# Divides moved behind the maxima in the short experts, and two output biases added by a matmul of 33 rows

## The chip, the core and the metric

The kernel runs on one core of a Trainium2 chip. The core has five engines: TensorE (PE, with its weight loads PEld), VectorE (DVE), ScalarE (ACT), GpSimd (POOL) and SyncE (SP), which here only issues DMAs. They run side by side and wait for each other on semaphores. The metric is the device time of one execution in microseconds (us), as the median of several executions.

## What is computed

A graph layer is followed by a layer of four experts. Each of 1250 rows goes to two of the four, and an expert attends only over the rows it was given. Cut to what matters here:

```python
def _expert(xf, mask, ln1_w, ln1_b, ipw, ipb, opw, opb, ln2_w, ln2_b, w1, b1, w2, b2):
    h = _ln(xf, ln1_w, ln1_b)
    q, k, v = jnp.split(h @ ipw.T + ipb, 3, axis=-1)      # 8 heads of 64 columns
    scores = jnp.einsum('htd,hsd->hts', q, k) / jnp.sqrt(D)
    a = jax.nn.softmax(jnp.where(mask[None, None, :], scores, NEG), axis=-1)
    o = jnp.einsum('hts,hsd->htd', a, v).transpose(1, 0, 2).reshape(T, E)
    o = o @ opw.T + opb
    x1 = xf + o
    h2 = _ln(x1, ln2_w, ln2_b)
    m = jax.nn.gelu(h2 @ w1.T + b1, approximate=False) @ w2.T + b2
    return x1 + m
```

The two output biases of the title are `opb` and `b2`, each 512 numbers added to every row.

## The kernel before

The graph layer comes first and takes 332 us. Routing follows, up to 421.5 us: it ranks the rows, makes a list for each expert, and scatters the rows into the lists in DRAM. Then the four experts run one after the other. An expert's rows are tiles of 128. What code an expert runs (its "arm") depends on how many tiles it has. Experts 0, 1 and 3 have four tiles here and run a **short** arm, written out without loops. In experts 0 and 1 the four tiles form two groups of queries, of 128 and of 384 columns (`nq` is 2); in expert 3 they form one group of 512 (`nq` is 1). Expert 2 has ten tiles and runs a **long** arm with a loop over pairs of heads.

Heads are numbered u = 0 to 7 and come in pairs j = u // 2. For a head, TensorE makes scores (L1481) of which VectorE takes each row's maximum (`maxima_of`, L2143, then L2147), TensorE turns the maxima into a row (L1492), ScalarE copies it (L1037), TensorE makes the scores again, transposed and less the maxima (L1506, L1508), ScalarE takes the exponentials (L1057), and TensorE sums values with them (L1522). ScalarE copies sums and denominators out to `o_pair` and `den` (L1049, L1050), and VectorE divides (`divide_of`: L2157 to L2160) into `oT`. Between these, TensorE projects the queries and keys of the pairs to come (`side_of`, L1467), ScalarE adds their bias (L1029, L1031) and VectorE splits them into a high and a low half (`split_of`, L2125 to L2129) and copies the second head's part (`second_of`, L2134 and L2135).

The engines' programs are fixed lists, so the order of the code is the order of the work. In TensorE's `short_head(u)` the first two scores of head u+1 stand early; the third has to wait until VectorE has read the first, because only two banks hold scores. So when VectorE is late with head u+1's first maximum, TensorE stops inside head u. VectorE's order in the short arm is `short_pair(j)`, printed below. After it `divide_of(3, s)` closes the heads, and the out-projection starts.

GpSimd makes the low halves of the weights from ScalarE's high halves (L562), copies values, and adds the biases: a DMA fills `row_par` with a bias on all 128 partitions, `add_bias` adds `opb` to the expert's input rows `x1` (L697) while the heads run, and after the second layer norm has read a tile GpSimd adds `b2` to it (L789). VectorE's `residual` waits for the first (`s_xb`), and its `part` for the second (`s_b2`).

`product(bank, lhs, rhs, chunks)` is TensorE's matmul in float16 halves, three passes over the chunks: 12 matmuls for a tile of the out-projection, 6 for a tile of the last product. An expert's tail is the out-projection (`project_out`), residual, layer norm, two products with the GELU between them, and the sum into `total_rows`. In the profile `x1` and other views of one memory are called `x_mem`.

Of the kernel before, what the change touches and what calls it, by code (L numbers as in the profile page):

```python
# [8 lines left out]
ALU = mybir.AluOpType  # L9
# [45 lines left out]
SHORT = 512  # L55
UP = 5
# [97 lines left out]
def program(nc, x, src, dst, gnn_w, gnn_par, gate_w, gate_b, ew, epar_d, erow, out):  # L154
    stack = ExitStack()
    with stack:
# [132 lines left out]
        row_par = sb("row_par", [P, D], F32)  # L289
# [103 lines left out]
        s_xb = sem("s_xb")  # L393
# [29 lines left out]
        s_b2 = sem("s_b2")  # L423
# [37 lines left out]
        def _(sp):  # L461
# [48 lines left out]
            sp.wait_ge(s_econst, 10)  # L510
# [8 lines left out]
            def expert_sp(e, shape):  # L519
# [26 lines left out]
                biased.skip(nt)  # L546
                sp.wait_ge(s_xb, biased.at(0))
                sp.sem_inc(s_idle, 1)
                sp.dma_start(row_par[:, :], erow[bass.ds(e, 1), 1, :].partition_broadcast(P)).then_inc(s_rp, 16)
                biased.settle()  # L550

            load_rows(0)
            biased = Tally(sp, "sp_biased", 0)
# [4 lines left out]
        def _(pool):  # L558
# [87 lines left out]
            nc.gpsimd.memset(total_rows[:, :, :], 0.0).then_inc(s_econst, 1)  # L646
            pool.wait_ge(s_power, 1)
# [20 lines left out]
            normed = Tally(pool, "pool_normed", 0)  # L668
# [7 lines left out]
            def expert_pool(e, shape):  # L676
# [45 lines left out]
                if shape.short:  # L722
# [7 lines left out]
                    add_bias()  # L730
# [14 lines left out]
                else:  # L745
# [5 lines left out]
                    add_bias()  # L751
# [26 lines left out]
                for p in range(shape.np):  # L778
# [6 lines left out]
                    if p == 0:  # L785
                        pool.wait_ge(s_rp, e * 32 + 32)
# [4 lines left out]
                normed.skip(nt)  # L791
# [16 lines left out]
                for r in (copied, stats, normed, summed, added, gathered, splits, returned_up, seconds):  # L808
                    r.settle()
# [1575 lines left out]
```

## Time and profile before

| what | value |
|---|---|
| median of 3 runs (lowest to highest) | 1335.82 us (1334.84 to 1337.59) |
| the profiled execution | 1336.74 us |
| its span | 1334.7 us |
| granted TensorE clock, mean | 0.884 |
| chain that ended last, by engine | PE 62%, DVE 16%, issue 11%, ACT 5%, POOL 3% |

| stretch, us | what | length | PE busy | DVE busy | ACT busy | POOL busy | clock |
|---|---|---|---|---|---|---|---|
| 332.0 to 421.5 | routing | 89.50 | 29.53 | 38.06 | 18.59 | 54.06 | 0.52 |
| 421.5 to 577.9 | expert 0, short | 156.40 | 111.19 | 100.15 | 72.20 | 58.67 | 0.87 |
| 577.9 to 725.8 | expert 1, short | 147.90 | 108.11 | 95.29 | 64.90 | 53.95 | 0.87 |
| 725.8 to 1173.1 | expert 2, long | 447.30 | 383.87 | 271.89 | 177.81 | 77.28 | 0.93 |
| 1173.1 to 1334.7 | expert 3, short | 161.60 | 122.62 | 86.53 | 57.01 | 40.59 | 0.88 |

The span is what the profiler saw of one execution, and the execution's own time is 2.0 us longer. Busy time is time in which an engine was inside an instruction. The clock is the share of 2.4 GHz that TensorE was granted: 1.0 is 2.4 GHz and 0.5 is 1.2 GHz. A row of a timeline below gives the start and the length of an instruction, or of several alike in a row (x4), and in brackets how long the engine had been idle and which engine's instruction ended that.

### The profile page before, as it was taken

Reading aid. Unit: us, or ns where it says so; the run is one execution under the profiler, and the core shown is the slowest. Engines: PE = TensorE matmul, PEld = TensorE weight load, DVE = VectorE, ACT = ScalarE, POOL = GpSimd, SP = SyncE. Lnnn points to the kernel's source line nnn. Section 1 sums busy time; section 2 is a strip of 40 time slices with the busy share of each in tenths; the row PEclk is TensorE's granted clock in tenths of the full one; section 3 lists DMA queues with packets and bytes.
Section 4 is the critical chain, followed back from the end, with each engine's and each line's share of the span. In section 5 each row is a group of like instructions: output and inputs, shape, how many; then the busy total and the mean of one; then the engine's idle time right before and its main releaser. Section 6 shows DMA issues by size and latency. Waiting matters only on the chain.

```text
span 1334.7 us, 19087 instructions
## 1 busy us (share of the span) xinstructions
PE 1025.8 (77%) x4940; PEld 571.0 (43%) x4941; DVE 749.8 (56%) x1557; ACT 453.7 (34%) x843; POOL 375.2 (28%) x340
## 2 busy tenths in 40 slices
PE   1987699998801876677776888979799779978874
PEld 1654477777800333333334433434344335533323
DVE  5395425441462368745685465674856537835654
ACT  1301121221312355234625423434434452235522
POOL 2102324441366163414342033000000125413212
PEclk9987799998555988889977888989999989989978
DMA  4291000000427114221333010000000312110010
GB/s 147 62 292 43 1 2 0 0 0 1 156 66 236 70 48 146 66 85 32 111 108 123 6 61 4 1 0 0 0 0 7 113 48 64 66 63 1 9 31 33
DMA packets 33792, 76.71 MB, mean 57 GB/s; under 512 B 6373, under 2 KB 6671, under 8 KB 33433
## 3 DMA queue, kind: packets, MB, share of 16 engines
q1 hardware_dynamic: 25405, 58.05, 14.0%
q0 software_dynamic: 8000, 15.44, 4.0%
q10 hardware_dynamic: 288, 2.10, 0.4%
q8 instruction: 39, 0.64, 0.2%
q14 instruction: 60, 0.49, 0.1%
HBM read 52.72 MB, written 24.13 MB: 58 GB/s over the span
## 4 chain that ended last, share of the span: by engine, by line
PE 62%; DVE 16%; issue 11%; ACT 5%; POOL 3%; DMA 1%; DVEq 1%; SPq 0%; ACTq 0%; POOLq 0%
PE bank L1346 14%; PE bank L1437 8%; PE bank L1221 8%; PE bank L1260 5%; PE bank L1467 4%; PE bank L1522 3%; PE bank L1256 2%; PE bank L1401 2%; PE bank L1422 2%; PE bank L1424 2%; PE bank L1187 2%; DVE den L2157 2%; POOL lists L658 1%; PE bank L1481 1%; PE bank L1506 1%
## 5 line engine op out<-in xcount | busy, mean ns | idle before, releaser
L1795 DVE TENSOR_SCALAR oh_src<-iota,edge 125x1250 f16 x178 | 101.8, 572 | 107.1 <-PE bank L1221 102.3
L1437 PE MATMUL bank<-probs_t,v_head 128*128 128x512 f32 (+1 forms) x288 | 148.5, 600 | 7.0 <-ACT probs_t L1006 6.4
L1006 ACT ACTIVATE probs_t<-bank 128x512 f32<-128x512 f32 x144 | 81.5, 573 | 141.6 <-PE bank L1424 141.1
L562 POOL TENSOR_TENSOR w<-w_stage,w 128x1024 f16<-128x1024 f32 x40 | 86.7, 2182 | 146.4 <-ACT w L819 146.4
L2080 DVE TENSOR_REDUCE mx<-bank 128x1 f32<-128x512 f32 x144 | 88.1, 656 | 69.6 <-PE bank L1401 69.0
L1221 PE MATMUL bank<-oh_src,oh_dst 125*125 x534 | 112.0, 361 | 2.7 <-DVE oh_dst L1797 0.7
L1522 PE MATMUL bank<-probs_t,v_head 128*128 128x128 f32 (+2 forms) x192 | 90.2, 555 | 7.7 <-ACT probs_t L1057 6.0
L1346 PE MATMUL bank<-hT,w 128*128 128x256 f16 (+1 forms) x552 | 89.5, 326 | 1.6 <-DVE hT L2013 1.6
L1221 PEld LDWEIGHTS bank<-oh_src,oh_dst 125*125 x534 | 71.1, 143 | 43.7 <-issue 24.6
L1346 PE MATMUL bank<-w,oT 128*128 128x512 f16 x264 | 67.3, 421 | 26.4 <-DVE oT L2160 17.3
L1467 PE MATMUL bank<-hT,w 128*128 128x512 f16 x288 | 76.6, 401 | 7.8 <-ACT t L1031 7.8
L1057 ACT ACTIVATE probs_t<-bank 128x128 f32<-128x128 f32 (+2 forms) x96 | 44.7, 487 | 100.1 <-PE bank L1508 99.6
L1346 PE MATMUL bank<-w,hT 128*128 128x512 f16 x264 | 66.2, 407 | 8.5 <-DVE hT L2013 8.5
L1346 PEld LDWEIGHTS bank<-hT,w 128*128 128x128 f16 (+1 forms) x552 | 57.1, 104 | 33.3 <-issue 3.0
L1354 PE MATMUL bank<-ident,probs_t 128*128 128x128 f32 x88 | 17.4, 354 | 67.9 <-ACT probs_t L946 59.5
L1437 PEld LDWEIGHTS bank<-probs_t,v_head 128*128 128x128 f32 x288 | 53.8, 198 | 29.9 <-ACT probs_t L1006 14.7
L2125 DVE TENSOR_TENSOR halves<-t,halves 128x512 f16<-128x512 f32 x24 | 17.7, 736 | 86.1 <-ACT t L1031 86.1
L684 POOL COPY v_head<-x_in 128x640 f32 x6 | 4.3, 722 | 217.0 <-PE bank L1437 217.0
L2143 DVE TENSOR_REDUCE mx<-bank 128x1 f32<-128x128 f32 (+2 forms) x96 | 48.9, 552 | 27.8 <-PE bank L1481 26.9
L1401 PE MATMUL bank<-k_hi,q_hi 66*128 66x512 f16 x144 | 44.9, 386 | 25.2 <-DVE mx L2080 14.2
L819 ACT CAST w<-w_stage 128x1024 f16<-128x1024 f32 x40 | 40.8, 1043 | 49.3 <-DMA w_stage<-in_ew_dram 48.9
L1422 PE MATMUL bank<-q_hi,k_hi 97*128 97x512 f16 x144 | 55.1, 383 | 2.7 <-ACT q_hi L984 2.7
(300 smaller groups left out, 1978.3 us busy)
## 6 DMA issues: line engine op xcount, KB each, us to landing
w_stage<-in_ew_dram SPq DMA_DIRECT2D x40, 512.0 KB, 3.8
lists<-zeros SPq DMA_DIRECT2D x1, 10340.0 KB, 50.0
x_in<-lists SPq DMA_DIRECT2D x20, 517.0 KB, 6.5
x_mem<-lists SPq DMA_DIRECT2D x3, 1024.0 KB, 8.3
x_mem<-lists SPq DMA_DIRECT2D x1, 2560.0 KB, 11.5
out_dram<-x_mem SPq DMA_DIRECT2D x10, 250.0 KB
big<-in_x_dram SPq DMA_DIRECT2D x10, 224.0 KB
x_mem<-in_x_dram SPq DMA_DIRECT2D x1, 2240.0 KB
```

The lines of the kernel that those rows point to most:

```text
L562: nc.gpsimd.tensor_tensor(w16[:, 1, cols], w_stage[:, p % WB, :], w16[:, 0, cols], ALU.subtract).then_inc(s_elo, 1)
L1006: nc.scalar.activation(probs_t[:, x % NPB, 0:cn], stb[x % 2][:, 0:cn], ACT.Exp).then_inc(s_exp, 1)
L1221: last = nc.tensor.matmul(ab[k][0:TT, 0:cn], oh_dst[:, bass.ds(slot, 1), i, :], oh_src[:, bass.ds(slot, 1), i, c0:c0 + cn], start=False, s ...
L1260: last = nc.tensor.matmul(b_h[i][:, 0:BW], w[:, j, feats], a[:, j, bass.ds(b * BW, BW)], start=False, stop=(k == 2 and j == NT - 1))
L1346: last = nc.tensor.matmul(bank, lhs(a, c), rhs(b, c), start=(n == 0 and c == 0), stop=(n == 2 and c == chunks - 1))
L1401: nc.tensor.matmul(sbk[i % 2][:, 0:cn], q_hi[0:MARK + 2, hd, t * P:(t + 1) * P], k_hi[0:MARK + 2, hd, c0:c0 + cn], start=True, stop=True). ...
L1422: nc.tensor.matmul(stb[i % 2][:, 0:cn], k_hi[0:SHIFT + 1, hd, kt * P:(kt + 1) * P], q_hi[0:SHIFT + 1, hd, c0:c0 + cn], start=True, stop=False)
L1437: nc.tensor.matmul(pvb[(hd * nq + s) % 2][:, 0:cn], v_head[:, hd, kt, :], probs_t[:, (hd * nx + i) % NPB, 0:cn], start=(k == 0), stop=(k = ...
L1467: last = nc.tensor.matmul(pp[0][:, 0:nt * P], w16[:, a, c0:c0 + P], hT[b][:, c, 0:nt * P], start=k == 0, stop=k == 3 * KC - 1)
L1522: nc.tensor.matmul(pvb[(hd * nq + s) % 2][:, 0:cn], v_head[:, hd, j % 2 * nt + kt, :], probs_t[:, i, 0:cn], start=(k == 0), stop=(k == nk ...
L1795: nc.vector.tensor_scalar(oh_src[:, bass.ds(slot, 1), i, 0:N].rearrange("p a n -> p (a n)"), iota[:, :], edge[:, 0, i, bass.ds(g, 1)], Non ...
L2080: nc.vector.tensor_reduce(mx[:, hd, t, s:s + 1], sbk[i % 2][:, 0:cn], AX.X, ALU.max).then_inc(s_mx, 1)
```

## The change

In the short arm, VectorE does both divides of a pair right behind the maxima of the next pair's second head. Before, the last of them (the only one where `nq` is 1) stood at the end of `short_pair`, right ahead of the maxima of head 2j+3.

The biases leave GpSimd. A DMA brings `opb` and `b2` to one partition each of `den` (0 and 32), once the expert before has given its memory back (`s_given`). VectorE's new `bias_halves` makes their high and low halves in rows 0 and 32 of `bias_rows`. Each `product` of the out-projection and of the last layer begins with one more matmul, of `ones_k` (33 rows of ones) and `bias_rows`, whose other rows are zero. ScalarE waits for `s_bias` before its first exponential in either arm, and GpSimd sets two more constants in the routing.

```diff
@@ SP, expert_sp
-                sp.dma_start(row_par[:, :], erow[bass.ds(e, 1), 0, :].partition_broadcast(P)).then_inc(s_rp, 16)
                 list_rows = lists[bass.ds(e * LIST, nt * P), 0:D].rearrange("(t p) d -> p t d", p=P)
                 sp.dma_start(x1[:, 0:nt, :], list_rows).then_inc(s_xr, 16)
+                sp.wait_ge(s_given, e + 1)
+                for b in range(2):
+                    sp.dma_start(den[LOW * b:LOW * b + 1, 0:D], erow[bass.ds(e, 1), b, :]).then_inc(s_rp, 16)
...
@@ POOL
             nc.gpsimd.memset(total_rows[:, :, :], 0.0).then_inc(s_econst, 1)
+            nc.gpsimd.memset(bias_rows[:, :], 0.0).then_inc(s_econst, 1)
+            nc.gpsimd.memset(ones_k[:, :], 1.0).then_inc(s_econst, 1)
...
-                def add_bias():
-                    pool.wait_ge(s_xr, e * 16 + 16)
-                    pool.wait_ge(s_rp, e * 32 + 16)
-                    for t in range(nt):
-                        nc.gpsimd.tensor_tensor(x1[:, t, :], x1[:, t, :], row_par[:, :], ALU.add).then_inc(s_xb, 1)
...
-                    add_bias()
...
-                    pool.wait_ge(s_n2, normed.at(2 * p + 2))
-                    for t in (2 * p, 2 * p + 1):
-                        nc.gpsimd.tensor_tensor(x1[:, t, :], x1[:, t, :], row_par[:, :], ALU.add).then_inc(s_b2, 1)
@@ ACT, short arm
-                    act.wait_ge(s_given, e + 1)
+                    act.wait_ge(s_bias, e + 1)
                     for u in range(H):
                         short_head(u)
@@ ACT, long arm
+                    act.wait_ge(s_bias, e + 1)
                     with nc.scalar.Fori(0, H // 2 - 1) as j:
@@ PE
-            def product(bank, lhs, rhs, chunks):
+            def product(bank, lhs, rhs, chunks, bias=None):
+                if bias is not None:
+                    nc.tensor.matmul(bank, ones_k[0:LOW + 1, :], bias, start=True, stop=False)
...
@@ DVE
+                def bias_halves():
+
+                    dve.wait_ge(s_rp, e * 32 + 32)
+                    for b in range(2):
+                        raw, cols = den[LOW * b:LOW * b + 1, 0:D], slice(b * D, (b + 1) * D)
+                        step(nc.vector.tensor_copy(bias_rows[0:1, cols], raw))
+                        last = nc.vector.tensor_tensor(bias_rows[LOW:LOW + 1, cols], raw, bias_rows[0:1, cols],
+                                                       ALU.subtract)
+                    last.then_inc(s_bias, 1)
@@ DVE, short_pair
                     maxima_of(2 * j + 1)
-                    if j > 0 and nq > 1:
-                        divide_of(j - 1, 0)
+                    if j > 0:
+                        for s in range(nq):
+                            divide_of(j - 1, s)
...
-                    if j > 0:
-                        divide_of(j - 1, nq - 1)
@@ DVE, short arm, and the same in the long arm behind second_head_copies()
                     second_of(0)
+                    bias_halves()
@@ DVE, residual and part
-                        dve.wait_ge(s_xb, biased.at(nt))
+                        dve.wait_ge(s_xr, e * 16 + 16)
-                    dve.wait_ge(s_b2, b2_done.at(t + 1))
```

The divides on VectorE, in the short arm with two groups, from the maxima of head 3 to those of head 5. Before (each "..." leaves out waits and rows of the same step):

```order
L2147 TENSOR_REDUCE neg_max<-mx 128x3
...
L2157 RECIPROCAL den<-den 128x128
...
L2125 TENSOR_TENSOR halves<-t,halves 128x512
L2126 COPY k_hi<-halves 64x512
...
L2143 TENSOR_REDUCE mx<-bank 128x1
...
L2129 COPY q_both<-halves 64x512
...
L2157 RECIPROCAL den<-den 128x384
...
L2143 TENSOR_REDUCE mx<-bank 128x1
```

The same stretch in the changed kernel (its line numbers are lower by 2 to 12):

```order
L2145 TENSOR_REDUCE neg_max<-mx 128x3
...
L2155 RECIPROCAL den<-den 128x128
...
L2155 RECIPROCAL den<-den 128x384
...
L2113 TENSOR_TENSOR halves<-t,halves 128x512
L2114 COPY k_hi<-halves 64x512
...
L2141 TENSOR_REDUCE mx<-bank 128x1
...
L2117 COPY q_both<-halves 64x512
...
L2141 TENSOR_REDUCE mx<-bank 128x1
```

The divide of 384 columns has gone from ahead of head 5's maxima to ahead of the split of the next pair's keys.

On TensorE, where the out-projection of the short arm begins; before:

```order
L1522 MATMUL bank<-probs_t,v_head 128x384
...
L1346 MATMUL bank<-w,oT 128x512 x12
L73 ISA
L1346 MATMUL bank<-w,oT 128x512 x12
...
L1645 MATMUL bank<-ident,probs_t 128x128 x8
```

and in the changed kernel:

```order
L1509 MATMUL bank<-probs_t,v_head 128x384
...
L1330 MATMUL bank<-bias_rows,ones_k 128x512
L1333 MATMUL bank<-w,oT 128x512 x12
L74 ISA
L1330 MATMUL bank<-bias_rows,ones_k 128x512
L1333 MATMUL bank<-w,oT 128x512 x12
...
L1633 MATMUL bank<-ident,probs_t 128x128 x8
```

Each tile of the out-projection has 13 matmuls in place of 12.

## Rows read from the trace of the kernel before

**Rows 1.** The page: busy time, share of the span and instructions of each engine.

```profile
PE 1025.8 (77%) x4940; PEld 571.0 (43%) x4941; DVE 749.8 (56%) x1557; ACT 453.7 (34%) x843; POOL 375.2 (28%) x340
```

**Rows 2.** Timeline of TensorE, expert 0: start, length, instruction, [idle before <-releaser].

```profile
481.35 0.97 PE L1481 MATMUL bank<-k_hi,q_hi 66*128 66x384 f16 x2 [5.14 <-DVE mx L2143]
482.11 1.91 PE L1467 MATMUL bank<-hT,w 128*128 128x512 f16 x4
...
489.32 0.23 PE L1506 MATMUL bank<-q_hi,k_hi 97*128 97x128 f16 x1 [0.40 <-ACT q_hi L1037]
...
491.34 0.38 PE L1481 MATMUL bank<-k_hi,q_hi 66*128 66x128 f16 x2
...
493.73 1.03 PE L1467 MATMUL bank<-hT,w 128*128 128x512 f16 x4
...
496.86 0.23 PE L1506 MATMUL bank<-q_hi,k_hi 97*128 97x128 f16 x1 [0.31 <-ACT q_hi L1037]
...
502.13 0.80 PE L1481 MATMUL bank<-k_hi,q_hi 66*128 66x384 f16 x2 [3.02 <-DVE mx L2143]
...
509.52 0.23 PE L1506 MATMUL bank<-q_hi,k_hi 97*128 97x128 f16 x1 [0.40 <-ACT q_hi L1037]
...
510.91 0.38 PE L1481 MATMUL bank<-k_hi,q_hi 66*128 66x128 f16 x2
...
515.77 0.23 PE L1506 MATMUL bank<-q_hi,k_hi 97*128 97x128 f16 x1
...
522.43 0.97 PE L1481 MATMUL bank<-k_hi,q_hi 66*128 66x384 f16 x2 [3.73 <-DVE mx L2143]
...
527.99 0.23 PE L1506 MATMUL bank<-q_hi,k_hi 97*128 97x128 f16 x1
```

**Rows 3.** Timeline of VectorE, expert 0: splits, divides, and both kinds stretched.

```profile
473.27 1.22 DVE L2125 TENSOR_TENSOR halves<-t,halves 128x512 f16<-128x512 f32 x1 [1.13 <-ACT t L1031]
474.42 1.35 DVE L2126 COPY q_hi<-halves 64x512 f16<-64x512 f16 x1
...
488.53 0.69 DVE L2125 TENSOR_TENSOR halves<-t,halves 128x512 f16<-128x512 f32 x1 [3.47 <-ACT t L1031]
...
497.59 2.55 DVE L2157 RECIPROCAL den<-den 128x384 f32<-128x384 f32 x1
...
508.73 0.69 DVE L2125 TENSOR_TENSOR halves<-t,halves 128x512 f16<-128x512 f32 x1 [3.06 <-ACT t L1031]
...
519.36 2.16 DVE L2159 TENSOR_SCALAR oT<-o_pair,ep 128x384 f16<-128x384 f32 x1
```

**Rows 4.** Timeline of GpSimd, expert 0: the bias on the input rows.

```profile
472.68 5.14 POOL L697 TENSOR_TENSOR x_mem<-x_mem,row_par 128x512 f32<-128x512 f32 x4 [0.34 <-POOL k_both L718]
```

**Rows 5.** Timeline of TensorE, expert 3: its three waits for maxima.

```profile
1226.66 0.39 PE L1481 MATMUL bank<-k_hi,q_hi 66*128 66x512 f16 x1 [2.55 <-DVE mx L2143]
...
1250.45 0.39 PE L1481 MATMUL bank<-k_hi,q_hi 66*128 66x512 f16 x1 [3.14 <-DVE mx L2143]
...
1270.71 0.39 PE L1481 MATMUL bank<-k_hi,q_hi 66*128 66x512 f16 x1 [1.66 <-DVE mx L2143]
```

**Rows 6.** Timelines of ScalarE and TensorE, expert 2: first exponential, wait for the second head.

```profile
792.64 0.60 ACT L1006 ACTIVATE probs_t<-bank 128x512 f32<-128x512 f32 x1 [1.29 <-PE bank L1424]
...
807.08 1.03 PE L1401 MATMUL bank<-k_hi,q_hi 66*128 66x512 f16 x2 [6.51 <-DVE k_both L2075]
```

**Rows 7.** Timeline of TensorE: out-projection of expert 0, tail of expert 2.

```profile
539.35 13.04 PE L1346 MATMUL bank<-w,oT 128*128 128x512 f16 x48 [5.24 <-DVE oT L2160]
...
1116.60 5.34 PE L1346 MATMUL bank<-w,oT 128*128 128x512 f16 x24
...
1151.47 1.47 PE L1645 MATMUL bank<-ident,probs_t 128*128 128x128 f32 x8 [2.87 <-DVE probs_t L2273]
```

**Rows 8.** Timelines of GpSimd and VectorE in the routing.

```profile
367.87 4.37 POOL L646 MEMSET total_rows<- 128x5120 f32 x1
...
367.91 4.38 DVE L1884 CAST member_h<-member 125x80 f16<-125x80 f32 x1
```

More of the change, by code:

```diff
@@ L55 @@
 SHORT = 512
+LOW = 32
 UP = 5
@@ L288, in program @@
         t32 = sb("t32", [P, 2, 512], F32)
-        row_par = sb("row_par", [P, D], F32)
+        bias_rows = sb("bias_rows", [P, 2 * D], F16)
+        ones_k = sb("ones_k", [P, P], F16)
         ep_ln1 = sb("ep_ln1", [P, 2 * KC], F32)
@@ L392, in program @@
         s_oT = sem("s_oT")
-        s_xb = sem("s_xb")
         s_l2v = sem("s_l2v")
@@ L422, in program @@
         s_m2 = sem("s_m2")
-        s_b2 = sem("s_b2")
+        s_bias = sem("s_bias")
         s_part = sem("s_part")
@@ L508, in _ @@
             sp.wait_ge(s_arms, 1)
-            sp.wait_ge(s_econst, 10)
+            sp.wait_ge(s_econst, 12)
             def load_rows(e):
@@ L545, in expert_sp @@
                         load_piece(e + 1, p)
[L546 to L550, printed above, removed]
             load_rows(0)
-            biased = Tally(sp, "sp_biased", 0)
             for e, shape in chosen(nc, sp, "sp", arms):
@@ L667, in _ @@
             stats = Tally(pool, "pool_stats", 0)
-            normed = Tally(pool, "pool_normed", 0)
             gathered = Tally(pool, "pool_gathered", 0)
@@ L750, in expert_pool @@
                         low_weights(e, p)
-                    add_bias()
                     summed.settle()
@@ L807, in expert_pool @@
                 pool.sem_inc(s_given, 1)
-                for r in (copied, stats, normed, summed, added, gathered, splits, returned_up, seconds):
+                for r in (copied, stats, summed, added, gathered, splits, returned_up, seconds):
                     r.settle()
@@ L905, in _ @@
             act.wait_ge(s_routed, 1)
-            act.wait_ge(s_econst, 10)
+            act.wait_ge(s_econst, 12)
             act.sem_inc(s_taken, 2)
@@ L1314, in _ @@
             pe.wait_ge(s_routed, 1)
-            pe.wait_ge(s_econst, 10)
+            pe.wait_ge(s_econst, 12)
             pe.wait_ge(s_slots, 1)
@@ L1341, in _ @@
             PASSES = [(0, 0), (1, 0), (0, 1)]
-            def product(bank, lhs, rhs, chunks):
+            def product(bank, lhs, rhs, chunks, bias=None):
+                if bias is not None:
+                    nc.tensor.matmul(bank, ones_k[0:LOW + 1, :], bias, start=True, stop=False)
                 for n, (a, b) in enumerate(PASSES):
                     for c in range(chunks):
-                        last = nc.tensor.matmul(bank, lhs(a, c), rhs(b, c), start=(n == 0 and c == 0),
+                        last = nc.tensor.matmul(bank, lhs(a, c), rhs(b, c), start=(n == 0 and c == 0 and bias is None),
                                                 stop=(n == 2 and c == chunks - 1))
@@ L1631, in project_out @@
                     product(sbk[t % 2][:, :], lambda a, c: oT[a][:, c, t * P:(t + 1) * P],
-                            lambda b, c: w16[:, b, W_OUT + c * D:W_OUT + (c + 1) * D], KC).then_inc(s_attn, 1)
+                            lambda b, c: w16[:, b, W_OUT + c * D:W_OUT + (c + 1) * D], KC,
+                            bias_rows[0:LOW + 1, 0:D]).then_inc(s_attn, 1)
                 def turn_second(p):
@@ L1665, in narrow @@
                         product(pvb[t % 2][:, :], lambda a, c: hid[a][:, c, t * P:(t + 1) * P],
-                                lambda b, c: w16[:, b, W_2 + c * D:W_2 + (c + 1) * D], HID // P).then_inc(s_m2, 1)
+                                lambda b, c: w16[:, b, W_2 + c * D:W_2 + (c + 1) * D], HID // P,
+                                bias_rows[0:LOW + 1, D:2 * D]).then_inc(s_m2, 1)
                 early = 1 if shape.short and nq > 1 else 0
@@ L1671, in expert_pe @@
                 pe.wait_ge(s_taken, emptied)
+                pe.wait_ge(s_bias, e + 1)
                 pe.wait_ge(s_elo, e * NWP + NWP)
@@ L1969, in _ @@
             dve.wait_ge(s_epar, 17)
-            dve.wait_ge(s_econst, 10)
+            dve.wait_ge(s_econst, 12)
             dve.sem_inc(s_split, 2)
@@ L1984, in _ @@
             on = Tally(dve, "dve_on", 2)
-            biased = Tally(dve, "dve_biased", 0)
             heads = Tally(dve, "dve_heads", 1)
@@ L1995, in _ @@
             mixed = Tally(dve, "dve_m2", 0)
-            b2_done = Tally(dve, "dve_b2", 0)
             parts = Tally(dve, "dve_parts", 0)
-            counts = [heads, taken, seconds, steps, scored, maxed, scored_t, on, biased, affine, attn, x1_done, normed,
-                      turned, gelued, mixed, b2_done, parts, sides]
+            counts = [heads, taken, seconds, steps, scored, maxed, scored_t, on, affine, attn, x1_done, normed,
+                      turned, gelued, mixed, parts, sides]
             def step(ins):
@@ L2213, in expert_dve @@
                     second_head_copies()
+                    bias_halves()
                     for r in counts:
@@ L2318, in expert_dve @@
                         give(2 * k - 5)
-                for r in (biased, affine, attn, x1_done, turned, mixed, b2_done, parts, results):
+                for r in (affine, attn, x1_done, turned, mixed, parts, results):
                     r.skip(nt)
```

3 lines of the change are left out of this document (removed).

## The prediction, made before the changed kernel was run

> **What bounds the kernel now.** I read the page first: TensorE is busy 77% of the span [rows 1], so what counts is where it stops. In TensorE's timeline of a short expert it stops at the same three places each time. In expert 0 these are the waits of 5.14, 3.02 and 3.73 us for a maximum by VectorE [rows 2], and a fourth of 5.24 us follows for the last divide, ahead of the out-projection [rows 7]. Expert 1 repeats them; expert 3 has 2.55, 3.14 and 1.66 us [rows 5]. A wait costs more than its own length: four L1467 matmuls take 1.91 us behind the wait of 5.14 us and 1.03 us further on [rows 2], which are TensorE's two levels, 1.2 and 2.4 GHz. Over such a slow stretch I count some 2 us (0.9 us on these four alone). Then VectorE's timeline says what held it. Ahead of the first wait its split took 1.22 us where it takes 0.69 us elsewhere, and a copy 1.35 us, while GpSimd added the bias to the input rows for 5.14 us [rows 3, 4]. Ahead of the second stood a divide of 384 columns, which begins at 497.59 us and runs to 501.79 us [rows 3]. Ahead of the third stood the same divide, stretched to 7.6 us by GpSimd's weight work (its L2159 took 2.16 us, [rows 3]).
>
> **Place 1, head 2: the bias on GpSimd goes.** The split took 1.22 us for 0.69, the first of its three copies 1.35 us for 0.28, and the other two a little less than that one [rows 3]: 3.3 us together, of which I book 3.2 us in experts 0 and 1. GpSimd's next weights then start earlier, but ScalarE's cast holds them until 474.9 us, so they stretch the small `owners` work as they did before. About 1.9 us of wait remain, and I leave the slow stretch in. In expert 3 the wait is only 2.55 us [rows 5]. I take 1.3 us of it and 1.5 us of slow stretch, 2.8 us in all.
>
> **Place 2, head 4: no divide ahead of the maxima.** The head lasts from 496.86 to 509.52 us, 12.66 us, and the head before it, with as much work and no wait, from 489.32 to 496.86, 7.54 us [rows 2]. That is 5.1 us less. Expert 3: its 3.14 us [rows 5] and 1.5 us of slow stretch, 4.7 us less.
>
> **Place 3, head 6: the same.** It lasts 12.22 us, from 515.77 to 527.99, and head 5 lasts 6.25 us, from 509.52 [rows 2]. 6.0 us less. In expert 3 the wait was 1.66 us [rows 5]; with its slow stretch 3.0 us less. Behind it, the last divides follow VectorE's maxima of head 7 without a pause in expert 0, so they come earlier by about as much, and the wait of 5.24 us stays as it is.
>
> **The new wait.** The divides now stand ahead of `split_of(j+1, 1)`, and behind that split are the second head's copies, GpSimd's copies and TensorE's scores of head 2j+2. VectorE was idle 3.47 and 3.06 us there [rows 3], and the moved divide takes 4.2 us. For pair 2 the split starts 0.7 us late. Its result was there at 490.0 us and TensorE asked at 491.34 [rows 2], so 1.3 us of slack take that up, unless TensorE is quicker or GpSimd's weights (about 2.2 us each) fall on the split: 0 to 3.9 us, and to 6 us with a slow stretch; I take 1.5. For pair 3 TensorE runs without place 2's wait and asks 1.4 us into head 5, at 510.91 [rows 2], 8.8 us after head 4's start. VectorE then has both divides to do (about 6.2 us from 3.8 us on) and a split of 1.5 us, which ends at 11.5: a wait of 2.7 us and 1 of slow stretch, 3.7 us. In expert 3 a divide of 512 columns takes 5.35 us and the head is longer: 1.1 and 0.3 us.
>
> **`bias_halves`.** Four small operations of 512 columns, each no more than the split's 0.69 us [rows 3]: 1.9 to 2.8 us. In a short expert VectorE idles there for about 7 us, and ScalarE's first exponential came 2.7 us after the copies that now stand ahead of it, so 0.3 us show. The DMAs are no matter: the memory is given back some 20 us earlier. **In the long expert** they do matter. ScalarE began its exponentials at 792.64 us [rows 6], and TensorE did four key tiles before it had to wait until 807.08 us for the second head's copies. Those copies still follow GpSimd's weights (to 797.3 us) and then six copies of 0.49 us or less, since the bias is no longer added beside them. VectorE reaches 800.1 us, and 802.4 us behind `bias_halves`. Only then may ScalarE begin. Four tiles took 7.3 us from there, so TensorE is at 810.4 us, at full clock, where it was at 807.08 us and slow for another 1.9 us: 1.6 us lost (0 to 4).
>
> **The 33 rows.** 24 products took 5.34 us, 0.22 us each [rows 7]. A row count of 66 in place of 128 makes no product visibly shorter, so I take the full 0.22 us (0 below). In a short tail the out-projection runs without a break once it has started, with the first product slow (0.43 us): 4 matmuls, 1.1 us. Of the last product's four, 0.8 us count in experts 0 and 1, and 0.4 us in expert 3, where GpSimd's scatters set the end. The long tail gets 20, 4.3 us, of which the wait of 2.87 us [rows 7] hides about two: 3.7 us. GpSimd's L789, which goes, ran beside all this and nobody waited for it.
>
> **Routing.** Two more constants stand on GpSimd behind the one that takes 4.37 us for 5120 elements [rows 8], 0.85 ns each: 0.98 us more. VectorE's cast was held for 4.38 us by the first one [rows 8]. If the next operations are held too the whole 0.98 us counts, otherwise nothing; I take 0.5. The Trainium skill (SBUF — State Buffer, Who interferes with whom) says that an operation with two SBUF inputs contends only with a GpSimd operation that reads SBUF, and a constant only writes. The two that follow the cast are of that kind; by the page it would be 0.3 us and the whole sum 0.2 us lower. No row here separates them from the cast.
>
> **The sum.** Experts 0 and 1: -3.2 -5.1 -6.0 +1.5 +3.7 +0.3 = -8.8 us each. Expert 3: -2.8 -4.7 -3.0 +1.1 +0.3 +0.3 = -8.8 us. Short tails: 1.9 + 1.9 + 1.5 = 5.3 us. Long expert: 1.6 + 3.7 = 5.3 us. Routing: 0.5 us. Together -26.4 + 11.1 = -15.3 us. The profiled execution took 1336.74 us, so 1321.4 us. The median of the runs is 0.9 us below it: **1320.5 us**.
>
> **Rivals.**
> (a) *The last divides bind, 1331 us.* In experts 0 and 1 VectorE does its divides back to back behind head 7's maxima, which come only 3.4 us earlier at place 3, and each of GpSimd's weights holds one of their steps for 2.2 us. If they fall on the moved divides as well, pair 2's wait is 3.9 us. Experts 0 and 1 then gain 3.8 us each, not 8.8. For it speaks the L2159 of 2.16 us [rows 3]. The Trainium skill (the same page and section) says that whichever of the two engines starts first holds the shared port for its whole instruction and the other stops; the trace agrees, with 2.16 us.
> (b) *TensorE stays at 2.4 GHz, 1311 us.* With the waits gone the stretch of 1.91 us in place of 1.03 us [rows 2] goes at place 1 too, GpSimd's weights miss the splits, and the new waits are hidden: 3 us more in each short expert.
> (c) *Slower, 1345 us.* The moved divides starve TensorE before heads 4 and 6: waits of 3.9 and 3.4 us with slow stretches of 2 us each behind them, and place 3 worth 3.4 us. Experts 0 and 1 then gain nothing and expert 3 gains 2 us, while the 11 us of matmuls, `bias_halves` and routing stay. It takes new waits of 10 us or more in a short expert to get there; I book 5.2. Against it: VectorE's idle 3.47 and 3.06 us [rows 3] hide most of 4.2 us.
> (d) *The divide was not the block.* If those first maxima were late for another reason, places 2 and 3 stay. But `divide_of(j-1, 1)` ends at 501.79 us and the wait at 502.13 us, so I give this no more than its share of (a).
>
> **How the numbers follow.** Chances: the forecast 0.47 (1315 to 1326 us by the bounds of its terms), (a) with (d) 0.22, (b) 0.21, (c) 0.10. Leaving out (c) and the far ends of (a) and (b), the range is 1309 to 1333 us. About 0.2% (2.7 us) can be told from no change here. Faster by more than that: forecast and (b), and most of (a), 0.86. Within it 0.05. Slower 0.09.
>
> **What would show it.** In the new profile TensorE's waits for maxima in heads 4 and 6 should be gone, and the one in head 2 near 2 us. New waits should stand ahead of the first scores of heads 4 and 6, 1 to 4 us, ended by VectorE's split or its copies. VectorE's idle time ahead of `split_of(j+1, 1)` should be gone. In expert 2, ScalarE's first exponential should begin about 10 us later relative to the expert's start, and TensorE should lose its wait of 6.51 us. Out-projections should be longer by 0.22 us a tile. The forecast fails if the new waits pass 5 us each, or if ScalarE's wait for the biases is seen in the short experts.

## The result and the profile after

The changed kernel takes 1330.11 us (median of seven runs, 1324.4 to 1332.62) against 1335.35 us before: a ratio of 0.9946 (95% interval 0.9926 to 0.9966). It is faster, by 5.2 us and not by 15.3. The profiled execution took 1330.95 us, with a span of 1329.2 us.

The page of the profile answers [rows 1]: TensorE's share of the span is 78%, and its instructions are 44 more.

```profile
PE 1032.8 (78%) x4984; PEld 570.0 (43%) x4985; DVE 739.1 (56%) x1573; ACT 454.8 (34%) x843; POOL 322.5 (24%) x298
```

TensorE's timeline of expert 0 answers [rows 2]:

```profile
476.83 0.80 PE L1468 MATMUL bank<-k_hi,q_hi 66*128 66x384 f16 x2 [1.53 <-DVE mx L2141]
477.47 1.03 PE L1454 MATMUL bank<-hT,w 128*128 128x512 f16 x4
...
488.12 0.45 PE L1468 MATMUL bank<-k_hi,q_hi 66*128 66x128 f16 x2 [3.48 <-DVE k_both L2117]
488.40 1.36 PE L1454 MATMUL bank<-hT,w 128*128 128x512 f16 x4
...
507.02 0.61 PE L1468 MATMUL bank<-k_hi,q_hi 66*128 66x128 f16 x2 [2.52 <-DVE k_both L2117]
...
531.64 0.60 PE L1330 MATMUL bank<-bias_rows,ones_k 33*128 33x512 f16 x1 [4.67 <-DVE oT L2158]
```

Of the waits of 5.14, 3.02 and 3.73 us for maxima only 1.53 us are left, in head 2. In their place TensorE waits 3.48 and 2.52 us for the last copy of VectorE's split. VectorE's rows of the same time, and one of GpSimd's, show why (compare [rows 3]): both divides now stand ahead of the split (L2113), and beside GpSimd's weights (L559) the last step of the second divide takes 2.36 us, where the same step takes 0.62 us at 504.56 us.

```profile
480.29 2.55 DVE L2155 RECIPROCAL den<-den 128x384 f32<-128x384 f32 x1
...
483.92 2.36 DVE L2158 SCALAR_TENSOR_TENSOR oT<-o_pair,ep,oT 128x384 f16<-128x384 f32 x1
486.20 0.68 DVE L2113 TENSOR_TENSOR halves<-t,halves 128x512 f16<-128x512 f32 x1
...
487.39 0.60 DVE L2117 COPY k_both<-halves 64x512 f16<-64x512 f16 x1
```

```profile
483.54 2.32 POOL L559 TENSOR_TENSOR w<-w_stage,w 128x1024 f16<-128x1024 f32 x1 [6.99 <-ACT w L803]
```

In the long expert the pause of 6.51 us [rows 6] has gone, and ScalarE's first exponential waits for the bias halves instead, and TensorE for that exponential:

```profile
798.35 1.09 ACT L990 ACTIVATE probs_t<-bank 128x512 f32<-128x512 f32 x2 [11.41 <-DVE bias_rows L2131]
```

```profile
799.00 2.08 PE L1424 MATMUL bank<-probs_t,v_head 128*128 128x512 f32 x2 [10.05 <-ACT probs_t L990]
```

Each tile of the out-projection begins with the bias matmul, and one tile starts 3.01 us behind the other:

```profile
537.12 0.39 PE L1330 MATMUL bank<-bias_rows,ones_k 33*128 33x512 f16 x1
537.43 2.76 PE L1333 MATMUL bank<-w,oT 128*128 128x512 f16 x12
540.13 0.39 PE L1330 MATMUL bank<-bias_rows,ones_k 33*128 33x512 f16 x1
```

I cut both traces at the same events and took the differences. "Heads" is from TensorE's first transposed scores to the out-projection, "tail" from there to the start of VectorE's last addition into `total_rows`, and "between" the rest of an expert.

| part, us | before | after | measured | forecast |
|---|---|---|---|---|
| heads, expert 0 | 84.93 | 78.18 | -6.8 | -8.8 |
| heads, expert 1 | 84.79 | 75.59 | -9.2 | -8.8 |
| heads, expert 3 | 91.85 | 81.50 | -10.4 | -8.8 |
| short tails, three | 98.60 | 109.92 | +11.3 | +5.3 |
| long expert, heads | 311.66 | 312.34 | +0.7 | +1.6 |
| long expert, tail | 64.67 | 69.42 | +4.8 | +3.7 |
| between | | | +5.1 | 0 |
| up to expert 0 | 426.36 | 425.30 | -1.1 | +0.5 |
| span | 1334.7 | 1329.2 | -5.5 | -15.3 |

The heads came out as forecast in their sum (-26.3 against -26.4 us), though not place by place. The tails and the time between two experts took 12.2 us more than I had booked, of which the long expert's tail has 1.1.

### The profile page after: what moved, and what is told of

Same layout as the page of the kernel before. It is cut to its first block, busy times and chain, and to the rows that moved or that the text cites. A ratio compares the mean times of both kernels' runs of the same rounds, so it can differ in the third digit from the quotient of the medians.

```text
span 1329.2 us, 19107 instructions
## 1 busy us (share of the span) xinstructions
PE 1032.8 (78%) x4984; PEld 570.0 (43%) x4985; DVE 739.1 (56%) x1573; ACT 454.8 (34%) x843; POOL 322.5 (24%) x298
## 4 chain that ended last, share of the span: by engine, by line
PE 63%; DVE 15%; issue 10%; ACT 5%; POOL 3%; DMA 1%; DVEq 1%; SPq 0%; ACTq 0%; POOLq 0%
PE bank L1333 17%; PE bank L1424 9%; PE bank L1206 8%; PE bank L1245 5%; PE bank L1454 3%; PE bank L1509 3%; PE bank L1241 2%; PE bank L1409 2%; PE bank L1388 2%; PE bank L1411 2%; PE bank L1172 2%; DVE den L2155 2%; POOL lists L657 1%; PE bank L1468 1%; PE bank L1330 1%
## 5 line engine op out<-in xcount | busy, mean ns | idle before, releaser
L559 POOL TENSOR_TENSOR w<-w_stage,w 128x1024 f16<-128x1024 f32 x40 | 85.9, 2161 | 144.2 <-ACT w L803 144.2
L1509 PE MATMUL bank<-probs_t,v_head 128*128 128x128 f32 (+2 forms) x192 | 87.4, 542 | 7.1 <-ACT probs_t L1041 5.3
L1454 PE MATMUL bank<-hT,w 128*128 128x512 f16 x288 | 71.5, 380 | 7.8 <-ACT t L1015 7.8
L908 ACT ACTIVATE t<-bank,ep 128x256 f32<-128x256 f32 x44 | 21.3, 566 | 114.5 <-PE bank L1633 114.5
```

The costliest lines, as they stand in the source:

```text
L559: nc.gpsimd.tensor_tensor(w16[:, 1, cols], w_stage[:, p % WB, :], w16[:, 0, cols], ALU.subtract).then_inc(s_elo, 1)
L1454: last = nc.tensor.matmul(pp[0][:, 0:nt * P], w16[:, a, c0:c0 + P], hT[b][:, c, 0:nt * P], start=k == 0, stop=k == 3 * KC - 1)
L1509: nc.tensor.matmul(pvb[(hd * nq + s) % 2][:, 0:cn], v_head[:, hd, j % 2 * nt + kt, :], probs_t[:, i, 0:cn], start=(k == 0), stop=(k == nk ...
```

## The experiments

All were timed beside the kernel before, at 1335.5 to 1336.1 us. Line numbers are those of each kernel.

**One part at a time.** Two kernels: the divides moved and nothing else, and the biases by matmul and nothing else.

```diff
b_order_only, in the kernel before
-                    if j > 0 and nq > 1:
-                        divide_of(j - 1, 0)
+                    if j > 0:
+                        for s in range(nq):
+                            divide_of(j - 1, s)
...
-                    if j > 0:
-                        divide_of(j - 1, nq - 1)
c_bias_only, in the changed kernel: the same lines turned round
```

> The kernel before with only the divides moved; the biases stay on GpSimd. Theory 1 (the divides gain 5 to 6 us at each of places 2 and 3 and give back 3 to 5 us at each new wait; from the two traces -1.1, -4.0 and -6.8 us in experts 0, 1 and 3): 1323.5 us, faster than the changed kernel, with the wait of 5.1 us in head 2 still there. Rival (the gain in the heads needs GpSimd free of the bias, which then has its turn elsewhere and holds the divides): 1330 us or more, with VectorE's divides stretched in head 3.

> The changed kernel with only the divides put back to where they stood before. Theory 1 (in the heads GpSimd's bias cost 3.6 to 5.4 us per short expert, 14 us in all, but the matmuls cost 11.5 us in the short tails and 5 in the long expert, and the starts of the experts 5): 1341 us, slower than before. Rival (the bias part pays for itself as I forecast, 9 us of heads against 11 us): 1335 to 1337 us.

The divides alone: **1317.09 us**, 0.9853 (0.9839 to 0.9868), 19.1 us less than before and 13 us less than the changed kernel. The biases alone: **1340.74 us**, 1.0038 (1.0024 to 1.0052), slower than before, as theory 1 had it. The two differences add up to -14.5 us. The changed kernel has -5.2, so some 9 us are lost only when both are together. 8.2 us of that lie in the heads of the short experts (-19.7 and -14.8 us apart, -26.3 together). Expert 0 shows where (us, from one head's first transposed scores to the next's):

| expert 0 | head 2 | head 3 | head 4 | head 5 | head 6 |
|---|---|---|---|---|---|
| before | 15.36 | 7.54 | 12.66 | 6.25 | 12.22 |
| b_order_only | 15.31 | 8.92 | 7.55 | 9.47 | 6.63 |
| c_bias_only | 9.56 | 7.54 | 12.66 | 6.25 | 11.94 |
| changed | 9.56 | 12.78 | 7.56 | 10.20 | 6.29 |
| f_split_divide | 9.55 | 8.07 | 7.55 | 9.17 | 7.32 |

GpSimd's bias cost head 2 5.8 us. With it gone and the divides moved, head 3 is 5.2 us longer. With the bias still there the moved divides cost head 3 only 1.4 us, and those come from GpSimd's weights, which fall on the split's last copy:

```profile
492.50 0.45 PE L1481 MATMUL bank<-k_hi,q_hi 66*128 66x128 f16 x2 [1.29 <-DVE k_both L2129]
```

```profile
490.22 2.15 DVE L2129 COPY k_both<-halves 64x512 f16<-64x512 f16 x1
```

In expert 1 it is the same (head 3: 7.43 before, 7.39 with the divides alone, 11.11 changed), and in expert 3 with less (9.20, 9.20, 11.02).

The two parts draw on one reserve: VectorE's idle time ahead of that split. The split needs the projections that TensorE makes in head 2. With the bias on GpSimd, TensorE makes them in its slow stretch behind the wait, and VectorE idles for 3.47 us [rows 3]. In c_bias_only the slow stretch is gone, they come sooner after the maxima, and the same idle time is 1.45 us:

```profile
482.21 0.69 DVE L2113 TENSOR_TENSOR halves<-t,halves 128x512 f16<-128x512 f32 x1 [1.45 <-ACT t L1015]
```

A divide of 4.2 us then makes the split 2.7 us late, and not 0.7. In the changed kernel it also reaches into GpSimd's next weights, which begin 0.9 us into head 3, and these add 1.7 us (the 2.36 us above). So the split is 4.4 us late, and TensorE waits 3.48 us. In some of the kernels below, head 2 keeps a slow stretch although no bias is added beside it. In expert 1 of g_both it takes 11.24 us, not 9.56, and VectorE idles there for 3.07 us again. In expert 1 of a_rows128 it takes 11.23 us, the divide ends ahead of GpSimd's weights, which fall on one copy of the split, and the wait is 1.55 us.

**Is it the matmul that makes the new wait?** GpSimd adds the bias, but as the first work of each expert, the long one too, and the divides are moved:

```diff
e_bias_first, in b_order_only, GpSimd
+                pool.wait_ge(s_xr, e * 16 + 16)
+                pool.wait_ge(s_rp, e * 32 + 16)
+                for t in range(nt):
+                    nc.gpsimd.tensor_tensor(x1[:, t, :], x1[:, t, :], row_par[:, :], ALU.add).then_inc(s_xb, 1)
                 pool.wait_ge(s_vcopy, copied.at(0))
...
                     second_head(1)
-                    add_bias()
```

> b_order_only with one difference: GpSimd adds the output bias to x1 as its first work of an expert, where VectorE's copies for head 2 are not beside it; no bias matmul. Theory 1 (the gain at head 2 and the moved divide share one reserve: with TensorE 5 us earlier at head 3, VectorE's split comes too late by most of it): the wait of 5.1 us in head 2 falls to 1.5 us, a wait of 3.4 us ahead of head 4's scores takes its place in experts 0 and 1 (1.7 us in expert 3), heads 2 and 3 together gain only 1.9, 2.6 and 1.9 us, and the time is 1310.5 us. Rival (the bias matmul itself caused those new waits, by bias_halves or the rows that it keeps): head 2 gains 5 us in full and the time is 1303.

**1307.56 us**, 0.9779 (0.9755 to 0.9802). The new wait is there without any bias matmul, at its full size:

```profile
473.58 0.80 PE L1478 MATMUL bank<-k_hi,q_hi 66*128 66x384 f16 x2 [1.53 <-DVE mx L2140]
...
484.88 0.61 PE L1478 MATMUL bank<-k_hi,q_hi 66*128 66x128 f16 x2 [3.50 <-DVE k_both L2126]
```

So the rival falls. Theory 1 was a little too kind, too: heads 2 and 3 together take 23.2 and 23.6 us in experts 0 and 1 against 24.2 and 23.3 with the bias in its old place, so nearly all of head 2's gain was given back there. In expert 3 they gain 1.9 us as expected. The time came out 3 us below theory 1 all the same, and not by the heads alone, which are 2.7 us shorter in the three short experts than in b_order_only. In the long expert the heads are 9.0 us shorter and the start 8.8 us longer, and in the profiled execution expert 0 begins 5.3 us sooner, though the edit changes nothing ahead of it.

**The divide cut in two.** The reciprocal of the last group follows the split and the second head's copies, and the other three steps follow the maxima of head 2j+2:

```diff
f_split_divide, in the changed kernel, short_pair
-                    if j > 0:
-                        for s in range(nq):
-                            divide_of(j - 1, s)
+                    if j > 0 and nq > 1:
+                        divide_of(j - 1, 0)
+                    if j == 3:
+                        divide_of(j - 1, nq - 1)
                     if j < 3:
                         split_of(j + 1, 1)
                         second_of(j + 1)
+                        if j > 0:
+                            divide_of(j - 1, nq - 1, rest=False)
                         maxima_of(2 * j + 2)
+                        if j > 0:
+                            divide_of(j - 1, nq - 1, first=False)
```

> The changed kernel with the divide of the last group cut in two: its reciprocal follows split_of(j+1, 1) and second_of(j+1), and its other three steps follow the maxima of head 2j+2. The same work in another order. Theory 1 (nothing but the divides ahead of the split makes the new waits): the waits of 3.5 and 2.5 us ahead of the scores of heads 4 and 6 go, heads 3 and 5 take 7.5 and 6.3 us as before the change, and the time is 1330 - 8 - 6 - 2 = 1314 us. Rival (the reciprocal then makes the maximum of head 2j+2 late, so the wait only moves to heads 3 and 5's third scores): 1326 to 1330 us, with waits for a maximum in place of those for k_both.

**1323.69 us**, 0.9914 (0.9893 to 0.9935): 6.4 us of the 16 expected. Both theories are half right. Ahead of head 4's scores no wait is left, and head 3 takes 8.07 us. Ahead of head 6's the wait has moved to a maximum, as the rival said, and in expert 3 heads 5 and 6 take 2.4 and 0.6 us longer than in the changed kernel:

```profile
485.62 0.38 PE L1468 MATMUL bank<-k_hi,q_hi 66*128 66x128 f16 x2
...
504.58 0.34 PE L1468 MATMUL bank<-k_hi,q_hi 66*128 66x384 f16 x1 [1.84 <-DVE mx L2141]
```

**The price of the 33 rows.** Only the slice of `ones_k` and `bias_rows` differs; the added rows are zero.

```diff
a_rows128, in the changed kernel (k_rows64 and l_rows66: 0:64 and 0:66)
-                    nc.tensor.matmul(bank, ones_k[0:LOW + 1, :], bias, start=True, stop=False)
+                    nc.tensor.matmul(bank, ones_k[:, :], bias, start=True, stop=False)
```

> The changed kernel with one difference: the bias matmul takes all 128 rows of ones_k and bias_rows (the rows beside 0 and 32 are zero), not 33. The result is the same. Theory 1 (a 33-row weight load between 128-row ones cannot run ahead, so each bias matmul costs a tile 0.42 us and not 0.22): a tile of the out-projection takes 2.81 us in place of 3.02, a tile of the last product 1.51 in place of 1.72, and 44 of them give back 7 to 9 us, some of it hidden: 1323 us. Rival (any matmul more, or the change of the weights' memory, costs 0.42 us): tiles stay at 3.02 us and the time at 1330.

> The changed kernel with a bias matmul of 64 rows in place of 33 (the added rows are zero). Theory 1 (up to 64 rows are a narrower mode of the array, and the change to it and back stops the run-ahead of the weight load): a tile of the out-projection takes 3.02 us as with 33 rows. Rival (the cost grows as the rows differ from 128, or it is the reading of one and the same weights that costs): 2.81 to 2.9 us.

> The changed kernel with a bias matmul of 66 rows (the added rows are zero), the row count of the score matmuls. Theory 1: 66 rows are in the mode of 128, a tile takes 2.81 us. Rival: 2.9 to 3.02 us, as any count beside 128.

**1322.49 us** with 128 rows, 0.9891 (0.9875 to 0.9908), 7.6 us less than with 33. With 64 and with 66 rows there is one execution each, 1330.27 and 1321.98 us. TensorE's rows of one tile and the start of the next, with 128, 64 and 66 rows:

```profile
537.56 0.38 PE L1330 MATMUL bank<-bias_rows,ones_k 128*128 128x512 f16 x1
537.78 2.75 PE L1333 MATMUL bank<-w,oT 128*128 128x512 f16 x12
540.37 0.38 PE L1330 MATMUL bank<-bias_rows,ones_k 128*128 128x512 f16 x1
```

```profile
537.76 0.39 PE L1330 MATMUL bank<-bias_rows,ones_k 64*128 64x512 f16 x1
538.08 2.76 PE L1333 MATMUL bank<-w,oT 128*128 128x512 f16 x12
540.77 0.39 PE L1330 MATMUL bank<-bias_rows,ones_k 64*128 64x512 f16 x1
```

```profile
538.45 0.38 PE L1330 MATMUL bank<-bias_rows,ones_k 66*128 66x512 f16 x1
538.67 2.75 PE L1333 MATMUL bank<-w,oT 128*128 128x512 f16 x12
541.26 0.38 PE L1330 MATMUL bank<-bias_rows,ones_k 66*128 66x512 f16 x1
```

From one tile's start to the next: 3.01 us with 33 and with 64 rows, 2.81 with 66 and with 128. The 12 matmuls alone took 2.59 us, by the start of the one behind them. A bias matmul costs 0.22 us with more than 64 rows and 0.42 us with 64 or fewer: 0.10 us more behind it (0.32 to the next start and not 0.22) and 0.10 us more ahead of the next one. All three runs are as theory 1 had them. TensorE's weight loads in the changed kernel have gaps at just those two places, both with "issue", and none within a tile that runs at full clock:

```profile
537.11 0.09 PEld L1330 LDWEIGHTS bank<-bias_rows,ones_k 33*128 33x128 f16 x1 [0.54 <-issue]
537.43 2.27 PEld L1333 LDWEIGHTS bank<-w,oT 128*128 128x128 f16 x12 [0.23 <-issue]
540.13 0.09 PEld L1330 LDWEIGHTS bank<-bias_rows,ones_k 33*128 33x128 f16 x1 [0.42 <-issue]
```

With 128 rows both gaps are gone:

```profile
537.56 2.47 PEld L1333 LDWEIGHTS bank<-w,oT 128*128 128x128 f16 x12
540.15 0.10 PEld L1330 LDWEIGHTS bank<-bias_rows,ones_k 128*128 128x128 f16 x1
540.37 2.47 PEld L1333 LDWEIGHTS bank<-w,oT 128*128 128x128 f16 x12
```

The Trainium skill (TensorEngine Tiling (Array Packing), Tiling Modes, Key Properties) says that a change of the tiling mode drains TensorE, and lists 64 rows as a mode of its own. The runs agree in where the step lies, between 64 and 66 rows, and a change there and back costs 0.2 us. That a drain fills the two gaps is not shown.

**The time between experts.** SyncE loads `x1` behind the two small bias transfers:

```diff
d_rows_later, in the changed kernel, SyncE
-                list_rows = lists[bass.ds(e * LIST, nt * P), 0:D].rearrange("(t p) d -> p t d", p=P)
-                sp.dma_start(x1[:, 0:nt, :], list_rows).then_inc(s_xr, 16)
                 sp.wait_ge(s_given, e + 1)
                 for b in range(2):
                     sp.dma_start(den[LOW * b:LOW * b + 1, 0:D], erow[bass.ds(e, 1), b, :]).then_inc(s_rp, 16)
+                list_rows = lists[bass.ds(e * LIST, nt * P), 0:D].rearrange("(t p) d -> p t d", p=P)
+                sp.dma_start(x1[:, 0:nt, :], list_rows).then_inc(s_xr, 16)
```

> The changed kernel with one difference: SyncE issues the transfer of the expert's input rows x1 behind the two small bias transfers (some 3 us later), not ahead of them. Theory 1 (between two experts the engines wait for instructions, whose transfers queue behind those rows, which now come 0.6 us earlier than before): the three pauses of VectorE fall from 5.57, 7.30 and 4.89 us to 5.1 or less, TensorE's pause of 3.89 us at the start of expert 2 goes, and the time falls by 3 to 5 us: 1326 us. Rival (the pauses come from where the code lies, or change from run to run): pauses as they were, 1330 us.

**1327.73 us**, 0.9939 (0.9927 to 0.9952), against 0.9946 (0.9926 to 0.9966): the medians are 2.4 us apart, but the intervals overlap, so the time alone settles nothing. The traces of this one edit say more. VectorE's last addition of expert 1 and its first operation of expert 2, before, changed, and with the later load, each with SyncE's transfer of `x1` (2.5 MB):

```profile
719.97 0.75 DVE L2294 SCALAR_TENSOR_TENSOR total_rows<-bank,share,total_rows 128x512 f32<-128x512 f32 x1 [0.54 <-PE bank L1346]
725.83 0.18 DVE L2031 COPY ep<-epar 128x30 f32 x1 [5.11 <-issue]
723.09 0.40 SPq L535 DMA_DIRECT2D x_mem<-lists  x1
```

```profile
711.88 0.75 DVE L2292 SCALAR_TENSOR_TENSOR total_rows<-bank,share,total_rows 128x512 f32<-128x512 f32 x1 [0.97 <-PE bank L1333]
719.93 0.18 DVE L2019 COPY ep<-epar 128x30 f32 x1 [7.30 <-issue]
714.45 0.41 SPq L535 DMA_DIRECT2D x_mem<-lists  x1
```

```profile
707.75 0.75 DVE L2292 SCALAR_TENSOR_TENSOR total_rows<-bank,share,total_rows 128x512 f32<-128x512 f32 x1 [0.97 <-PE bank L1333]
713.47 0.18 DVE L2019 COPY ep<-epar 128x30 f32 x1 [4.96 <-issue]
712.98 0.41 SPq L538 DMA_DIRECT2D x_mem<-lists  x1
```

The pause is 7.30 us when `x1` is sent 2.57 us behind that addition's start, 5.11 us at 3.12, and 4.96 us at 5.23. The other traces agree: 6.93 to 7.30 us in all seven kernels that send it at 2.6 us, 4.68 to 5.11 in the five that send it at 3.1 to 3.7, and 5.14 in j_matmul_best, which sends it at 5.8. TensorE's pause at the start of expert 2 fell from 3.89 to 2.35 us (3.20 before), and did not go. The profile's table of DMA queues has queues of kind "instruction" that work in this stretch. That these transfers wait behind the rows fits, but no run shows them one by one. The pause ahead of expert 1 did not follow: 4.71 us before, 5.57 changed, 5.37 here. Its 0.9 us, and up to 1.5 us in which expert 2 reaches its first scores later (65.66 us before, 67.14 changed, 66.53 here, 64.5 to 67.7 in the other kernels that load `x1` where the changed one does), stay open.

**The long expert's wait.** ScalarE waits for the bias halves only before it first writes `den`:

```diff
h_long_wait, in the changed kernel, ScalarE
-                    act.wait_ge(s_bias, e + 1)
                     with nc.scalar.Fori(0, H // 2 - 1) as j:
...
                     act.wait_ge(s_oT, free)
+                    act.wait_ge(s_bias, e + 1)
                     nc.scalar.copy(o_pair[mine, c0:c0 + cn], bank[mine, 0:cn])
```

> The changed kernel with one difference: in the long arm ScalarE waits for the bias halves just before it first overwrites den (inside copy_sums), not before its first exponential. Theory 1 (the early wait is what holds the long expert's first exponentials for 11 us): that pause goes, TensorE's first sums come 10 us earlier, but its stop for the second head's copies returns, so that only 1.5 to 2 us are gained: 1328 us. Rival (TensorE would have waited for those copies all the same until as late): 1330 us, nothing gained.

**1323.43 us**, 0.991 (0.9884 to 0.9936): 6.7 us gained where I expected 2. The long expert's heads fall from 312.34 to 304.96 us. My reason for the 2 was wrong. TensorE's stop for the second head's copies does not return, since these copies are fast once GpSimd no longer adds a bias beside them (e_bias_first, with no bias matmul, has 302.5 us for these heads). VectorE's copy of the keys' second head, before and changed:

```profile
800.03 1.38 DVE L2071 COPY k_hi<-halves 64x1280 f16<-64x1280 f16 x1
```

```profile
793.56 0.48 DVE L2059 COPY k_hi<-halves 64x1280 f16<-64x1280 f16 x1
```

**The best of both ways.** Without the bias matmul: g_both is e_bias_first with the divide cut in two, and i_best lets GpSimd add the long expert's bias only behind VectorE's copies. With it: j_matmul_best has all four repairs.

```diff
i_best, in g_both, GpSimd (the additions of g_both, now the function add_bias)
+                if shape.short:
+                    add_bias()
...
                     for p in range(QKV_P, NWP):
                         low_weights(e, p)
+                    pool.wait_ge(s_qkb, e * (H // 2) + 1)
+                    pool.sem_inc(s_idle, 1)
+                    add_bias()
```

> e_bias_first and f_split_divide together, without the bias matmul: GpSimd adds the bias first, and the divide is cut in two. Theory 1 (the three losses of the changed kernel, matmuls, new waits and the starts of the experts, are independent of each other once the shared reserve is no longer needed): e_bias_first less 4 to 5 us at head 3 and 3 to 4 at head 5 in experts 0 and 1 and 2 in expert 3: 1294 to 1298 us. Rival (GpSimd's weights fall on the reciprocal or the copies instead and keep a wait of 2 us each): 1304 us.

> g_both with one difference: in the long arm GpSimd adds the bias only after VectorE's second-head copies are done, and not first (in g_both that made the start of expert 2 last 70.3 us up to its first scores, against 64.2 in b_order_only). In the short arm it stays first. Theory 1 (both things that the bias can be in the way of, VectorE's split at the start and its copies for the second head, are then clear of it): expert 2 starts as in b_order_only and its heads stay at 302 us, so 5 to 6 us less than g_both: 1291 us. Rival (the 13 us of GpSimd's additions then hold VectorE's maxima or the next pair's split): 1297 us.

> The changed kernel with all four repairs: 128 rows, the divide cut in two, x1 loaded behind the biases, and ScalarE's wait for the biases inside copy_sums. Theory 1 (the losses are independent): 1330 - 7.6 - 6.4 - 2.4 - 6.7 = 1307 us, still some 15 us slower than i_best, since 44 matmuls remain, and the small bias work at the start of every expert. Rival (with the new waits gone, the rest is hidden behind VectorE's last divides): 1315 us.

g_both **1297.02 us**, 0.9707 (0.9688 to 0.9726); i_best **1292.66 us**, 0.9679 (0.9666 to 0.9692); j_matmul_best **1303.6 us**, 0.9764 (0.9751 to 0.9777). Against theory 1, g_both fell inside its 1294 to 1298 us, i_best 1.7 us above and j_matmul_best 3.4 us below. In i_best expert 2 reaches its first scores after 65.99 us (70.32 in g_both), and its heads take 302.01 us, 9.7 less than before. i_best computes the same as the kernel before with the same instructions: 43 us gained by order alone, 11 us more than with the best form of the bias matmul.

## Why the prediction was right or wrong

The sum was 9.8 us too good (-5.5 us measured, -15.3 forecast). The price of the 33 rows, in the tails, makes 7.1 us of it and the time between the experts, which I had put at nothing, 5.1 us; the long expert's heads and the part up to expert 0 gave back 0.9 and 1.6 us. In the short experts' heads two errors cancelled.

**Places 1 to 3: right, place 1 too small.** In expert 0 head 2 gained 5.8 us (3.2 booked; 5.0 in expert 1), head 4 5.1 (5.1) and head 6 5.9 (6.0); in expert 3 3.6, 5.3 and 3.9 (2.8, 4.7 and 3.0). Place 1 gave more since the slow stretch went with the wait: the four L1454 take 1.03 us. That part of rival (b) came true at place 1 alone. The waits for maxima went as forecast (1.53 us left in head 2, about 1.9 expected), which rules out (d).

**The new wait of pair 2: the step that failed in the heads.** I booked 1.5 us, because "1.3 us of slack take that up". It measured +5.2 and +3.7 us in experts 0 and 1, with waits of 3.48 and 3.44. My sum was the divide's 4.2 us less VectorE's idle 3.47 us, "the split starts 0.7 us late". But 2.0 us of that idle time came from TensorE's slow stretch in head 2. I had left that stretch in, and it went with the bias: the idle time is then 1.45 us (c_bias_only) and the divide 2.7 us late. GpSimd's weights add 1.7 us on L2158, so the split is 4.4 us late. I had named both, "unless TensorE is quicker or GpSimd's weights (about 2.2 us each) fall on the split", and still took 1.5 us of a range up to 3.9, as if neither would come. b_order_only shows that the slack was real as long as place 1 stayed (+1.4 and 0 us), and e_bias_first that it goes with it (3.50 us). The wait comes near rival (a)'s "pair 2's wait is 3.9 us". Pair 3 measured +3.9 and +3.2 us for 3.7, expert 3 +1.8 and +0.6 for 1.1 and 0.3. The heads' sum is right by luck: place 1 gave more than booked, and the new wait took it.

**(a)'s reason for place 3 did not come.** The last divides start early enough: head 6 gained 5.9 us, not 3.4, and the wait ahead of the out-projection went from 5.24 to 4.67 us, with a head 7 longer by 0.8 us in expert 0 and shorter by 0.2 in expert 1.

**The 33 rows: mis-sized by a factor of two.** "A row count of 66 in place of 128 makes no product visibly shorter, so I take the full 0.22 us." It is 0.42 us. I had asked only whether fewer rows could be cheaper and put the other bound at the nearest row, one with 66. The short tails took +11.3 us for 5.3, the long one +4.8 for 3.7. At 0.22 us each they are +3.6 to +5.0 and +1.2 to +2.9 (a_rows128, l_rows66, j_matmul_best), so at the right price my count of what shows would have been a little too high.

**Between the experts: not in my sum.** +3.4 us in VectorE's three pauses and +1.6 to the first scores. I wrote "the DMAs are no matter", having asked when the bias data arrive, but not what else SyncE's queue would then do sooner. The largest piece, 2.2 us ahead of expert 2, follows the moment at which `x1` is loaded; the rest is open.

**`bias_halves`: no wait for it is seen in the heads of the short experts, and in the long one a near hit by luck.** The long expert's heads took +0.7 us (1.6 booked), and ScalarE's first exponential came 11.6 us later relative to the expert's start (10 forecast; 66.81 us before, 78.42 now). But the early wait costs 7.4 us, and I saw only the difference to before: without it the long expert's heads are 6.7 us shorter than before (304.96 against 311.66), which the end of GpSimd's addition gives, and the wait took all of that.

**Routing: 0 for 0.5 us.** GpSimd's two constants run from 371.13 to 372.30 us, and VectorE's operations beside them keep their length:

```profile
371.13 1.01 POOL L644 MEMSET bias_rows<- 128x1024 f16 x1
372.08 0.22 POOL L645 MEMSET ones_k<- 128x128 f16 x1
```

```profile
371.31 0.35 DVE L1879 TENSOR_REDUCE best<-masked 125x10 f32<-125x40 f32 x2
371.70 0.17 DVE L1882 TENSOR_TENSOR gap<-best 125x10 f32<-125x10 f32 x1
```

The same two rows took 0.35 and 0.17 us before. The second has two inputs and runs beside a constant. So the rule of the Trainium skill (SBUF — State Buffer, Who interferes with whom) holds here: a constant does not hold an operation with two inputs. The 1.1 us that this part lost are not the change's; over the kernels of this study it ended between 421.1 and 427.0 us.

## What to carry to other kernels

Two waits that one engine has in a row may rest on the same reserve of another. When the first is removed, what ran slowly behind it gets faster, and the second engine's idle time, read from the old trace, shrinks. So work that idle time out again before you fill it, and do not add up two gains read from one trace. Where an addition stretches the busy engine's operations beside it, move it to where that engine is idle before you replace it by work on the engine that bounds the kernel, and give a small matmul between large ones more than 64 rows. A wait for data that is needed late belongs right ahead of the instruction that needs it.

## What the runs showed of the hardware

A float16 matmul of 33 or 64 rows between others of 128 rows costs 0.2 us more than one of 66 or 128 rows, although its own duration is 0.39 us for 0.38. And VectorE's pause at an expert's start depends on when a transfer of 2.5 MB is sent, by up to 2.3 us, though the profile shows no wait of it for that transfer. Beside GpSimd's addition VectorE's copy of 64x1280 float16 takes 1.38 us, without it 0.48 us.
